# The opening and the first two units of a bidirectional state-space layer, issued in another order

## The reference, cut to what matters

```python
h = table[ids]                                   # one gathered row per token
u = layernorm(layernorm(h), ln_g, ln_b)
x, gate = split(u @ in_w.T)                      # 128 channels each
act = silu(dwconv_causal(x, conv_w, conv_b))
def mamba(a):                                    # for act, and for act reversed
    x, z = split(a @ dir_in_w.T)
    x = silu(dwconv_causal(x, dir_conv_w, dir_conv_b))
    dt, B, C = split(x @ xproj_w.T)              # 8, 16, 16 columns
    dt = softplus(dt @ dt_w.T + dt_b)
    state = exp(dt * A) * state + (dt * x) * B   # 16 states a channel, step by step
    y = sum(state * C) + x * D
    return (y * silu(z)) @ dir_out_w.T
h = h + (concat(mamba(act), mamba(reversed)) * silu(gate)) @ out_w.T + u
h = h + experts(layernorm(h))
```

## Time and profile before

| what | us |
|---|---|
| median of 3 runs | 554.12 (553.49 to 556.9) |
| the profiled execution | 556.38 |
| its span | 554.6 |

### The profile page before, as it was taken

One profiled execution on the slowest core, in us unless ns is written; L12 is line 12 of the kernel. 1 busy time (PEld: TensorE's weight loads), 2 busy tenths in 40 slices (PEclk: granted clock), 3 DMA queues, 4 the chain that ended last, 5 costly groups with the idle time before them and its releaser, 6 DMA issues.

```text
span 554.6 us, 5648 instructions
## 1 busy us (share of the span) xinstructions
PE 463.7 (84%) x1651; PEld 180.5 (33%) x1651; DVE 484.3 (87%) x599; ACT 375.3 (68%) x660; POOL 473.1 (85%) x152
## 2 busy tenths in 40 slices
PE   2987886788979797979898898978997996795987
PEld 1433322323323242424233433333333332232433
DVE  3576785989999899999999999999999999999951
ACT  1478385777777778785977588768776785474633
POOL 5352589898998989899999999999999999999810
PEclk9999797997989898999999899999898998696999
DMA  4158484726163451707172717171726271700000
GB/s 60 13 51 253 89 247 71 240 80 242 58 199 108 137 172 36 261 31 240 68 233 77 240 60 252 66 251 59 226 92 234 75 243 47 258 18 9 0 11 19
DMA packets 50401, 71.05 MB, mean 128 GB/s; under 512 B 15891, under 2 KB 16835, under 8 KB 50371
## 3 DMA queue, kind: packets, MB, share of 16 engines
q1 hardware_dynamic: 47378, 69.36, 38.0%
q0 software_dynamic: 1024, 1.05, 3.4%
q10 hardware_dynamic: 1968, 0.29, 0.3%
HBM read 60.19 MB, written 10.49 MB: 127 GB/s over the span
## 4 chain that ended last, share of the span: by engine, by line
PE 37%; DVE 28%; issue 14%; POOL 10%; ACT 8%; SPq 1%; DMA 1%; DVEq 0%; POOLq 0%; ACTq 0%
DVE st L1538 15%; POOL st L490 8%; DVE st L1523 6%; PE ps L626 6%; PE ps L713 3%; PE ps L688 3%; PE ps L725 3%; PE ps L601 2%; POOL st L481 2%; PE ps L807 2%; PE ps L823 2%; ACT ps L1089 2%; PE ps L653 2%; ACT L989 1%; PE ps L665 1%
## 5 line engine op out<-in xcount | busy, mean ns | idle before, releaser
L490 POOL TENSOR_TENSOR st<-st,repC 128x2048 f32<-128x2048 f32 x63 | 285.3, 4535 | 18.4 <-ACT carry L1095 13.5
L1538 DVE TENSOR_TENSOR_SCAN st<-ps,carry,st 128x512 f32<-128x512 f32 x192 | 234.8, 1267 | 4.8 <-ACT ps L1089 4.2
L1089 ACT ACTIVATE ps<-dtS,negA 128x512 f32<-128x512 f32 x256 | 170.9, 681 | 48.2 <-DVE st L1538 47.0
L481 POOL TENSOR_TENSOR st<-duS,repB 128x2048 f32<-128x2048 f32 x30 | 136.1, 4537 | 0.0
L1538 DVE TENSOR_TENSOR_SCAN st<-ps,zero,st 128x512 f32<-128x512 f32 x64 | 78.9, 1270 | 7.7 <-ACT ps L1089 7.4
L713 PE MATMUL ps<-st,fold 128*32 128x512 f32 x504 | 69.6, 625 | 15.2 <-POOL st L490 15.0
L1523 DVE TENSOR_TENSOR st<-duS,ps 128x2048 f32<-128x2048 f32 x33 | 75.0, 2272 | 3.4 <-PE ps L688 3.2
L626 PE MATMUL ps<-act,wT 128*128 128x512 f32 x128 | 57.8, 594 | 0.3 <-ACT act L1032 0.3
L462 POOL DMA_INDIRECT x<-in_L_tok_ple_table,idx x32 | 30.5, 952 | 31.9 <-DMA dtS<-dt_dram 13.1
L688 PE MATMUL ps<-xr,Bw 128*128 128x512 f32 x68 | 39.2, 660 | 10.7 <-ACT bc_sb L1081 6.0
L665 PE MATMUL ps<-xr,wT 128*32 128x512 f32 x32 | 20.5, 726 | 21.7 <-DVE st L1523 21.7
(11 more groups left out here) (143 smaller groups left out, 636.4 us busy)
## 6 DMA issues: line engine op xcount, KB each, us to landing
dtS<-dt_dram SPq DMA_DIRECT2D x64, 256.0 KB, 4.3
duS<-du_dram SPq DMA_DIRECT2D x64, 256.0 KB, 3.5
repC<-bc_dram SPq DMA_DIRECT2D x64, 256.0 KB, 5.0
repB<-bc_dram SPq DMA_DIRECT2D x30, 256.0 KB, 3.1
dt_dram<-dt SPq DMA_DIRECT2D x16, 256.0 KB, 3.1
du_dram<-du SPq DMA_DIRECT2D x16, 256.0 KB, 2.0
bc_dram<-bc_sb SPq DMA_DIRECT2D x16, 64.0 KB, 4.9
out_h<-fin SPq DMA_DIRECT2D x8, 128.0 KB, 2.0
```

Source lines behind the costliest of these rows:

```text
L481: pool.tensor_tensor(st[:, r], duS[:, u % 2], row, ALU.mult).then_inc(sem("dbu_pool"), 1)
L490: pool.tensor_tensor(st[:, r], st[:, r], row, ALU.mult).then_inc(sem("hc_ready"), 1)
L1089: sc.activation(decay_bank(u, r, q), dtS[:, u % 2, q], ACT.Exp, scale=negA[:, way(u), q, r:r + 1]).then_inc(sem("decay_ready"), 1)
L1538: dve.tensor_tensor_scan(st[:, r, q, order], decay_bank(u, r, q)[:, order], st[:, r, q, order], first, ALU.mult, ALU.add).then_inc(sem("sc ...
```

## The change

What is computed stays the same. The lists are rewritten for the opening, unit 0 and unit 1.

- DMA: dt and du of unit 0 are spread straight out of SBUF; their stores to DRAM are gone. `D` and `Alog` of both directions form a list of their own behind the other weights (`rest_loads`), with `dir_ow` in direction b's list. The experts' weights (`late_loads`) move from before unit 0's loop to the end of unit 1's turn.
- POOL: gathers 0 to 7 run before the masks, 8 to 21 without a wait, 22 to 31 behind `du_first_0`; none is left in unit 0. `dt_times_x(2)` moves behind `input_product(1, 2)`.
- PE: chunk 0's and chunk 1's products interleave ahead of dt; zero products stand at other places; `skip_product(0)` and one zero product move from before `sum_dt(1)` to before `conv(2)`; row 1 of B of unit 0 goes to bank Y, so that it doesn't wait for row 0; `pre(3)` and `sum_dt(3)` move back within unit 1.
- DVE and ACT: norms 1 to 3 square on DVE, norms 0 and 1 are chained before the rest; unit 0's softplus is split over both engines in another form; in unit 1 the softplus of unit 3 is spread over positions 4 to 7 (`second_unit`), and `conv_silu(4)` goes to the end of its burst.

```diff
@@ loads
-            ld.append((dir_ow[:, d], A(n + "_out_w")))
-            ld.append((dskip[:, d:d + 1], col(A(n + "_D"))))
+            rest_loads.append((dskip[:, d:d + 1], col(A(n + "_D"))))
...
-                ld.append((alog[:, d, q, :], rows.unsqueeze(1).broadcast_to([32, 4, NS])))
+                rest_loads.append((alog[:, d, q, :], rows.unsqueeze(1).broadcast_to([32, 4, NS])))
@@ SP
-                sp.wait_ge(sem("dt_in_dram"), 16)
-                spread(dtS[:, 0, q, :], dt_dram[0][rows]).then_inc(sem(f"dt_first_{q}"), 16)
-                sp.wait_ge(sem("du_in_dram"), 16)
-                spread(duS[:, 0, q, :], du_dram[0][rows]).then_inc(sem(f"du_first_{q}"), 16)
+                sp.wait_ge(sem("dt_ready"), 1)
+                spread(dtS[:, 0, q, :], dt[rows]).then_inc(sem(f"dt_first_{q}"), 16)
+                sp.wait_ge(sem("du_ready"), 1)
+                spread(duS[:, 0, q, :], du[rows]).then_inc(sem(f"du_first_{q}"), 16)
             store_bc(0)
-            store_dt(0)
-            store_du(0)
             for q in range(NQ):
                 first_quarter(q)
@@ POOL
-            for t in range(TC):
+            for t in range(2 * TC):
                 gather(t)
...
-            pool.wait_ge(sem("x_ready"), 1)
-            for t in range(TB, TB + 4):
+            for t in range(2 * TC, TB + 6):
+                gather(t)
+            pool.wait_ge(sem("du_first_0"), 16)
+            for t in range(TB + 6, TILES):
                 gather(t)
@@ PE, the opening and unit 0
             dt_weights(0, 7)
             way_b_weights()
-            write_nought(1, 0)
+            write_nought(1, LONG)
             turn_chunk(0)
+            write_nought(1, 1)
+            x_chunk(0, 1)
+            gate_chunk(0, 0)
+            turn_chunk(1)
+            conv(0, 1)
+            x_chunk(1, 0)
+            pre(0)
             dt_weights(1, 9)
...
             bc(0)
+            conv(1, 1)
             b_rows(0, 0)
             pre(1)
             bc(1)
-            skip_product(0)
-            add_nought(3)
+            write_nought(2, Y)
+            turn_chunk(2)
+            write_nought(2, Y)
             turn_chunk(3)
             b_rows(0, 1)
             sum_dt(1)
+            b_rows(0, 2)
             x_chunk(2, LONG)
-            b_rows(0, 2)
             x_chunk(3, ZED)
+            skip_product(0)
+            add_nought(1)
             conv(2, PRE)
...
@@ ACT
+            def first_abs():
+                sc.wait_ge(sem("sp_a"), 1)
+                sc.activation(e_[:], ps[:, PRE, :], ACT.Abs, bias=dt_b[:, 0:1]).then_inc(sem("sp_a"), 1)
...
-                if u + 3 < UNITS:
+                if 1 != u < UNITS - 3:
                     conv_silu(u + 3, PRE)
                 for v in zeds(u):
                     z_silu(v, ZED)
...
+                if u == 1:
+                    conv_silu(4, PRE)
...
+            def second_unit(p):
+                if p == 3:
+                    dt_out(2)
+                if p == 4:
+                    softplus_in(3)
+                if p == 5:
+                    softplus_exp(3)
+                if p == 6:
+                    softplus_plus1(3)
+                    softplus_ln(3)
+                if p == 10:
+                    dt_out(3)
@@ ACT, the opening
             uT_chunk(0)
+            rsqrt(1)
             silu_tables()
             act_silu(0, 1)
+            gate_silu(0, 0)
+            uT_chunk(1)
+            conv_silu(0, 1)
+            act_silu(1, 0)
+            exp_ln_tables()
+            first_abs()
+            softplus_exp(0)
+            first_plus1()
+            first_ln()
             sc.wait_ge(sem("dtproj_ps"), 2)
             out_of_psum(dtproj[:, 1, :], ps[:, 2, 2 * P:3 * P], "dtproj_ready")
+            bc_out(0)
+            silu_tables()
+            conv_silu(1, 1)
             exp_ln_tables()
+            decay_rates(0)
+            decay_rates(1)
             rsqrt(2)
             rsqrt(3)
@@ ACT, unit 0
+                if p == 12:
+                    bc_out(2)
+                    softplus_in(2)
                 if p == 13:
                     keep_last(0, 2)
-                    softplus_in(2)
+                    softplus_exp(2)
                 if p == 14:
-                    softplus_exp(2)
                     softplus_plus1(2)
-                if p == 15:
                     softplus_ln(2)
-                    bc_out(2)
@@ DVE, unit 0 and unit 1
                 if p == 2:
+                    start_residual(2)
+                if p == 3:
                     log1p_error(1)
+                    input_product(0, 1)
                     start_residual(3)
...
+                if p == 7:
+                    if u == 1:
+                        log1p_error(3)
```

More of the change, by code:

```diff
@@ L424, in _ @@
             load_C(1)
-            with nc.allow_non_contiguous_dma(reason="b1 is 2 KB"):
-                for dst, src in late_loads:
-                    sp.dma_start(dst, src).then_inc(sem("late_in"), 16)
             for u in range(UNITS):
@@ L442, in _ @@
                     load_dt(u + 2)
+                if u == 1:
+                    with nc.allow_non_contiguous_dma(reason="b1 is 2 KB"):
+                        for dst, src in late_loads:
+                            sp.dma_start(dst, src).then_inc(sem("late_in"), 16)
             store_out(UNITS - 2)
@@ L471, in dt_times_x @@
                 pool.wait_ge(sem("dt_ready"), u + 1)
-                wait(pool, "du_in_dram", 16 * u)
+                if u == 1:
+                    for q in range(NQ):
+                        pool.wait_ge(sem(f"du_first_{q}"), 16)
+                else:
+                    pool.wait_ge(sem("du_in_dram"), 16 * (u - 1))
                 pool.wait_ge(sem("x_ready"), u + 1)
@@ L509, in _ @@
                     by_c(u - 1, NR - 1)
-                if u == 1:
-                    dt_times_x(2)
                 if u == 0:
-                    pool.wait_ge(sem(f"dt_first_{NQ - 1}"), 16)
-                    for t in range(TB + 4, TB + 12):
-                        gather(t)
                     dt_times_x(1)
@@ L523, in _ @@
                 by_c(u, 2)
-                if u == 0:
-                    for t in range(TB + 12, TILES):
-                        gather(t)
                 if 0 < u < UNITS - 2:
@@ L543, in turn, with write_nought @@
                 return pe.transpose(ps[0:m, bank, at:at + k], src, ident[0:k, 0:k])
+            def write_nought(n, bank):
+                for _ in range(n):
+                    pe.matmul(ps[:, bank, :], nought[:], nought[:].unsqueeze(1).broadcast_to([P, TC, P]),
+                              start=True, stop=True)
+            pe.wait_ge(sem("idx_ready"), 1)
+            pe.wait_ge(sem("pads_ready"), 1)
+            write_nought(2, LONG)
             pe.wait_ge(sem("taps_ready"), 1)
@@ L889, in _ @@
                     bc(u + 2)
-                if u + 2 < UNITS:
+                if u == 1:
+                    pre(3)
+                if u > 1 and u + 2 < UNITS:
                     sum_dt(u + 2)
@@ L911, in _ @@
                     partial(u - 1)
+                if u == 1:
+                    sum_dt(3)
                 if third:
@@ L1073, in dt_out @@
                 sc.wait_ge(sem("dt_ps"), u)
-                wait(sc, "dt_in_dram", 16 * u)
+                if u == 1:
+                    for q in range(NQ):
+                        sc.wait_ge(sem(f"dt_first_{q}"), 16)
+                else:
+                    sc.wait_ge(sem("dt_in_dram"), 16 * (u - 1))
                 sc.wait_ge(sem("du_ready"), u)
@@ L1514, in _ @@
             ch.mark(dve.tensor_copy(w1[DM:DM + E], maskf))
+            rates(0)
+            rates(1)
+            dve.wait_ge(sem("ln_log"), 4)
+            norm_newton(2)
+            start_u2(2)
             ch.wait()
```

198 lines of the change are left out of this document (95 added, 103 removed).

## The result

| | median, us | range of the runs | n |
|---|---|---|---|
| before | 555.59 | 553.08 to 556.9 | 14 |
| after | 558.8 | 557.89 to 560.37 | 14 |

The ratio is 1.0066 with an interval of 1.0045 to 1.0087: slower by 0.7%, within the 1% of the forecast's middle case, but on the other side of zero and above the range (545.0 to 556.5). A ratio compares the single runs, without those that took over 1.5% more than the fastest of the same kernel, so it isn't the ratio of the medians. The profiled execution spans 557.0, before 554.6.

A forecast was written before the change was run, and what follows sets the result against it. Behind 122.5 us DVE, then POOL, were taken to run without slack; ahead of it the gains left 3.0. Taken from the profiled 556.38 this gave 553.4, as a median 551.1; range 545.0 to 556.5.

The forecast's parts named there:

- the forecast's middle case: Whole kernel: time within one per cent (5.5 us) of before, between 548.6 and 559.7; chance 0.64.
- the gain at unit 2's first scan: End of unit 1: unit 2's first scan at 119.5 instead of 122.5, a gain of 3.0 us.
- The gain at the first scan: End of the opening: first scan of unit 0 at 43.0 instead of 49.51, a gain of 6.5 us.
- the rival of full clock: Units 0 and 1: PE runs both dt sums at 2.4 GHz, 4.0 us more gain, 547.1; chance 0.27.
- The head of the opening: Chunk 0: norm at 13.0 instead of 15.31, a gain of 2.3 us, with the norm's end at 17.3.
- The rival without a gain there: Opening: PE's list delays chunk 0's turn by 3.0 us, so all gain goes, 554.1; chance 0.17.
- Unit 0 gives gain back: Unit 0: the gain shrinks from 6.5 us at its first scan to 2.7 at unit 1's first scan.
- Unit 1: Unit 1: the removed 6.53 us wait comes back almost whole as a list handing on unit 3's dt; gain 3.0 remains.
- Spreads out of SBUF: Opening: eight spreads of unit 0's dt and du out of SBUF take 8.7 us, as fast as from DRAM.
- the slow rival: Unit 0, position 3: spreads three times as long (26 us) delay its scan, about 562.7; chance 0.07.

The follow-up runs named there:

- a_shift2: Changed kernel plus one idle DVE write of about 0.9 us ahead of unit 2's first scan; 558.35 us, ratio 0.9991 to the kernel before.
- a_warm: Changed kernel plus five more zero products in PE's pauses of units 6 to 9; 555.58 us, ratio 1.0003 to the kernel before.
- a_dram: Changed kernel with dt and du of unit 0 stored to DRAM and spread from there again; 558.15 us, ratio 1.0032 to the kernel before.
- b_again: The kernel before, run again unchanged; median 556.74 us, 12 runs from 553.87 to 560.9.
- a_swap_hot: Changed kernel with a_hot's zero products and conv(1) ahead of bc(0) on PE; 554.11 us, ratio 0.9969 to the kernel before.
- a_u1_hot: Changed kernel with a_hot's zero products and unit 1 in its old order; 555.44 us, ratio 0.9996 to the kernel before.
- a_sums: Changed kernel with five zero products ahead of sum_dt(1) and five instead of two ahead of sum_dt(2); 555.42 us, ratio 0.9942 to the kernel before.
- b_hot: The kernel before plus zero products in PE's pauses of units 2 to 13; 554.65 us, ratio 0.9990 to the kernel before.
- a_hot: Changed kernel plus the same zero products as b_hot in units 2 to 13; 556.55 us, ratio 1.0017 to the kernel before.
- a_again: The changed kernel, run again unchanged; 557.98 us, ratio 1.0030 to the kernel before.

## Why the prediction was wrong

**The step that failed** is the first: "Behind it DVE and then POOL run without slack that could swallow a shift, and neither gets other work. So I count the shift of unit 2's first scan at 122.5, and pass it to the end one for one." The lists behind unit 2 are the same, but their time is not a constant: 432.1 before and 436.2 after, and 438.4 in a second profile of before. It is the last of the prediction's signs of being wrong, a unit behind 122.5 that takes longer (unit 8: 31.1 for 29.5). PE has pauses in the units; which of them are followed by a fall differs with where unit 2 stands. The two short falls that before and a_shift2 have in units 6 to 9 cost nothing (112.5 and 112.6); the four of after, two of them twice as long, cost POOL what it doesn't make up. a_warm (the pauses filled: 112.4) and a_shift2 (the same list 0.9 later: 112.6) take the 4.1 away; a_dram and after, with one list up to the DMAs, have the same falls to 0.2 and 116.6. One number goes with the falls: in after and a_dram unit 2's first scan follows the return of the clock in unit 1 by 30.5 and 30.4 (90.3 to 120.8 and 89.3 to 119.7), in before by 31.2 (91.3 to 122.5), in a_shift2 by 31.3 (90.7 to 122.0). The runs of each pair have the same falls in units 2 to 9; b_again, at 31.5, already has others than before. Why these distances give these falls the trace doesn't show, and I leave it open.

**How the miss adds up.** From the forecast of 551.1 to the median of 558.8 it is 7.7. Of these, 4.1 are the step above; 1.3 are the gain at unit 2's first scan, 1.7 in the pair of profiles for 3.0. The last 2.3 are the step from a profiled execution to a median: the prediction took off the 2.26 by which before's profiled execution stood above the median of its first three runs, but after's took 558.8, just its median.

**Terms that were mis-sized.** The gain at the first scan was 6.5 in the forecast, 3.5 in the pair of profiles. dt came 1.7 late, and conv(0) was late by 1.6 already, 24.48 for 22.9: the two products ahead of it took 2.95, partly at half clock, where I had 1.8, and the gate and the turn of chunk 1, which stand between, I had left out. And conv(1) took 5.34, not 3.70, since I placed it behind `bc(0)`'s wait without asking what that wait does to PE's clock, although I asked it for the sums. a_swap_hot shows what that wait and the slow convolution cost together: 2.6 to 3.6 at the first scan. `sum_dt(2)` took 4.5 (86.2 to 90.7) for 3.7, and conv(4) ended at 112.3 for 110.9. In unit 0, 18.85 and 1.8 make 20.65, not 20.9; measured it was 20.5. And the clock of 0.61 at 84 to 86 in before, from which the rival of full clock took that not much is lacking, is the mean over a stretch in which the clock falls; behind it, to 91, it is 0.50:

```profile
86.00:88.00 2.00, 1.14 (x2) 0.65 (x3) 2.00 (x3) 1.43 (x4) 1.85 (x2) 0.50 0.13 33
```

**What came as forecast.** The head of the opening: norm at 13.4, turn at 17.7. The rival without a gain there falls, though not for the reason given: PE's list ahead of the turn wasn't shortened in its zero products, it has five for one, but it ran at full clock and was done in time. To that extent the outcome was luck. Unit 0 gives gain back, about half of what was forecast: it lasts 40.0 after, forecast 41.9, before 38.0. Unit 1 lasts 34.8 where I had 34.6, before 35.0, and a_u1_hot shows that its order earns nothing. Spreads out of SBUF took 13.4, under the 15 at which the slow rival would have decided, and no scan of unit 0 waited for them. The Trainium skill (SBUF — State Buffer, Door 1: The DMA port swizzle) says that 32 partitions reach only half the ports; the estimate from its figures was 5 more than 8.7, and the trace agrees in size, with 4.5 more than through DRAM. That the ports are the cause no run here shows. The rival of full clock in both sums had the right size at unit 2's first scan (a_sums: 3.5 for 4.0) but didn't happen by itself.

**The gain at unit 2 is smaller than one pair of profiles says.** Over three profiles of the list of before (before, b_again, b_hot) unit 2's first scan stands at 122.5, 120.6 and 121.5, mean 121.5; over five of the changed opening (after, a_warm, a_hot, a_dram, and a_shift2 without its 0.9) at 120.8, 121.7, 121.7, 119.7 and 121.1, mean 121.0. So 3.0 was forecast and about 0.5 arrives. The first scans stand at 48.9 and 45.7 in the mean, those of unit 1 at 86.7 and 86.0: of 3.2 gained in the opening unit 0 takes 2.6 back. Three and five profiles that lie up to 2 us apart make this 0.5 a rough figure.

**What stays open:** how large the loss is on the whole. Ratios of 1.0066, 1.0030 and (a_dram) 1.0032 were measured in three comparisons, only the first clear of zero, and over all of them the kernel before had medians from 555.0 to 558.6. That the falls are where the 4.1 of the two profiles went is shown; that every run of the changed kernel meets them is not (its shortest, 551.95, ran at a mean clock of 0.95), and before meets falls of its own, as b_again shows.

## What to carry to other kernels

A forecast that moves a start by a microsecond or two and takes the rest as fixed is only as good as the rest is: look first how far runs of one program lie apart and whether their mean clock goes with their time. A pause on PE can have two prices, the wait and the half clock behind it; fill the pause with work that is needed anyway (here a convolution, 2.6 to 3.6 at the first scan and 1.5 at unit 2) or with zero products (here 3.5 for two sums), and do it where something waits for the products behind. A shorter opening is worth what arrives where the bound engine becomes full, not what it is at the first scan (here 0.5 of 3.2 in the mean).

## What the runs showed of the hardware that I had not expected

The falls of PE's clock can repeat from run to run at the same places of the program to 0.2 (after, a_dram and a_again behind unit 2; the two profiles of before don't agree so far), and 0.9 of idle work on another engine moves them to other places: units 6 to 9 went from 116.6 to 112.6 by it. Single runs of one unchanged program spread over 7 us (553.87 to 560.9), in step with the mean clock (0.95 to 0.924). And eight spreads of 256 KB out of 32 partitions of SBUF took 13.4, longer than the same eight out of DRAM, 8.9 to 9.0.
